# The last cross attention gets its own order of work and a ring of eight rows

## The reference, cut to what matters

```
x = x + self_attn(layernorm(x))                 # per batch item: 224 x 512
q = layernorm(x) @ Wq + bq;  k = ctx @ Wk + bk;  v = ctx @ Wv + bv      # ctx: 750 x 512
att = (q k^T / sqrt(32)) * mask - 1e10 * (1 - mask)                     # 16 heads, 224 x 750
x = x + (softmax(att) @ v) @ Wo + bo
x = x + experts(layernorm(x))      # all 8 items together, gathers rows of the expert table
```

## Time and profile before

| | |
|---|---|
| median of 3 runs | 2667.64 us (2662.12 to 3053.95) |
| the profiled execution | 2672.23 us, its span 2670.4 us |
| mean granted TensorE clock | 0.963 of full speed |
| busy share of the span | TensorE 88%, VectorE 70%, ScalarE 44%, GpSimd 42% |
| last cross attention, first scores to last quad copied | 1297.8 to 1394.2 us, 96.4 us |
| in it, granted clock | 0.77 |

### The profile page before, as it was taken

One profiled execution on the slowest core, in us unless ns is written; L12 is line 12 of the kernel. 1 busy time (PEld: TensorE's weight loads), 2 busy tenths in 40 slices (PEclk: granted clock), 3 DMA queues, 4 the chain that ended last, 5 costly groups with the idle time before them and its releaser, 6 DMA issues. The chain is left out here.

```text
span 2670.4 us, 37760 instructions
## 1 busy us (share of the span) xinstructions
PE 2355.7 (88%) x12440; PEld 1263.5 (47%) x12440; DVE 1870.6 (70%) x5466; ACT 1185.9 (44%) x3230; POOL 1122.6 (42%) x1084
## 2 busy tenths in 40 slices
PE   7899999999999999999777799898989898897777
PEld 3455564555655556555554344444444344443322
DVE  3477676776768667677554896878878787878555
ACT  1447365573745737466351343343334333433322
POOL 2121111211112111121001676777777777777775
PEclk9899999999999999999878899999999999999999
DMA  5000101001010010100202998999999999999998
GB/s 179 8 24 8 37 2 30 16 8 38 1 45 1 8 38 1 45 1 22 93 1 85 372 391 335 399 401 418 395 416 397 410 409 399 400 395 395 407 416 355
DMA packets 161362, 520.73 MB, mean 195 GB/s; under 512 B 17168, under 2 KB 27408, under 8 KB 161168
## 3 DMA queue, kind: packets, MB, share of 16 engines
q0 software_dynamic: 129024, 469.82, 44.3%
q1 hardware_dynamic: 30560, 46.98, 5.3%
q10 hardware_dynamic: 1584, 1.52, 0.2%
HBM read 507.71 MB, written 10.55 MB: 194 GB/s over the span
## 5 line engine op out<-in xcount | busy, mean ns | idle before, releaser
L1593 POOL DMA_INDIRECT e_rows<-in_experts,e_idx x896 | 888.2, 991 | 340.9 <-issue 287.7
L1650 PE MATMUL e_ps_out<-e_rows,e_diag 128*128 128x512 f32 x1792 | 843.5, 617 | 145.3 <-ACT e_diag L1917 145.1
L1811 DVE CUSTOM_DVE_ANT_0 e_rows<-e_rows,xn_all 128x512 f32<-128x512 f32 x896 | 567.8, 689 | 232.0 <-DMA e_rows<-in_experts,e_idx 231.8
L1650 PEld LDWEIGHTS e_ps_out<-e_rows,e_diag 128*128 128x128 f32 x1792 | 343.8, 197 | 594.3 <-issue 428.5
L1917 ACT ACTIVATE e_diag<-ident_f,e_weight 128x128 f32<-128x128 f32 x896 | 286.2, 390 | 313.1 <-DVE e_weight L1822 297.6
L984 DVE SCALAR_TENSOR_TENSOR ring<-ps_s,mask 112x750 f32<-112x750 f32 x256 | 232.8, 936 | 152.7 <-PE ps_s L557 115.2
L1170 ACT ACTIVATE ring<-ring,neg_max 112x750 f32<-112x750 f32 x256 | 233.4, 914 | 165.3 <-DVE neg_max L994 165.3
L568 PE MATMUL ps_t<-ident,ring 112*125 112x112 f32 x1536 | 233.6, 290 | 47.9 <-ACT prob_t L1188 36.5
L568 PEld LDWEIGHTS ps_t<-ident,ring 112*125 112x125 f32 x1536 | 199.7, 196 | 122.9 <-ACT ring L1170 61.7
L1912 ACT ACTIVATE e_active<-e_hidden 128x4 f32<-128x4 f32 x224 | 45.9, 205 | 456.4 <-DVE e_hidden L1811 456.2
L1188 ACT COPY prob_t<-ps_t 125x336 f32<-125x336 f32 x512 | 200.1, 440 | 95.6 <-PE ps_t L568 95.4
(11 more groups left out here) (186 smaller groups left out, 2850.4 us busy)
## 6 DMA issues: line engine op xcount, KB each, us to landing
e_rows<-in_experts,e_idx POOLq DMA_INDIRECT x896, 6.2
xn_t<-in_ctx_t SPq DMA_DIRECT2D x8, 1500.0 KB, 6.5
w_in<-in_ffn_wq SPq DMA_DIRECT2D x16, 256.0 KB, 6.2
acc<-in_x SPq DMA_DIRECT2D x8, 448.0 KB, 5.0
x_dram<-x SPq DMA_DIRECT2D x8, 448.0 KB, 3.1
acc<-x_dram SPq DMA_DIRECT2D x7, 512.0 KB, 6.1
out<-acc SPq DMA_DIRECT2D x14, 256.0 KB, 5.9
x2n_dram<-ring SPq DMA_DIRECT2D x7, 448.0 KB, 3.3
```

The source lines that it names most:

```text
L1593: pool.indirect_dma_start(rows[:, v % RING, k, :], None, table[:, :], bass.IndirectOffsetOnAxis(ap=idx[:, e:e + 1], axis=0))\
L1650: mm = nc.tensor.matmul(ps_out[t % 2][:], diag[:, HU * (v % ND) + k, :], rows[:, v % RING, k, D:], start=(s == 0 and k == 0), stop=(s == S ...
L1811: last = nc.vector.tensor_tensor_reduce(down, down, xn_all[:, t, :], 1.0, 0.0, ALU.mult, ALU.add, hidden[:, b, k:k + 1])
```

## The change

Three things change, all in the last batch item.

- `cross(b, following)` on TensorE, VectorE and ScalarE now serves only the first seven items. The last has a function of its own, `last_cross`, on each of the three engines. TensorE issues a quad's first scores as the quad's first work, takes the last row of the quad before out of turn, and puts `cross_weigh` behind it. VectorE takes rows and masks in pairs. ScalarE alternates exponentials and copies. Of the 12 tiles turned ahead, VectorE copies six and ScalarE six.
- The last cross attention uses eight rows: six of `ring` and two in the memory of `w_v`, which the last `values_group` has read by then (`spare`, `cross_rows`, `ring_rows`). `spread_out` and `cross_bank` give the tail other banks, so that `cross_out` of tile 1 does not wait for tile 0's `residual_2`, and `spread_sums` goes ahead of the last `cross_weigh`.
- `with_bias` of the last item waits until both tiles of the turned rows are in `act_t`.

```
-NRING, NSELF = 6, 12
+NRING, NLAST, NSELF = 6, 8, 12
...
+        spare = w_v[:].rearrange("p c n -> p (c n)")[0:TT, 0:(NLAST - NRING) * SC].rearrange("p (i n) -> p i n", n=SC)
...
-            return ((bank[2], bank[3]), ps_t)[k][t]
+            return ((bank[2], bank[3]) if k == 0 or b == last else ps_t)[t]
...
+        def ring_rows(b):
+            return NLAST if b == last else NRING
+        def cross_bank(b, t):
+            return bank[0] if b == last and t == 1 else ps_y
+        def cross_rows(b, u, n):
+            i = u % ring_rows(b)
+            return ring[:, i:i + n, :] if i < NRING else spare[:, i - NRING:i - NRING + n, :]
...  TensorE
+            def last_cross():
+                for ready in q2_ready:
+                    pe.wait_ge(ready.sem, ready.at(last, KC // 2))
+                for q in range(NQ + 1):
+                    u = 4 * q - 4
+                    if q < NQ:
+                        cross_scores(last, q, 0)
+                    if q >= 2:
+                        cross_turn(last, u - 1)
+                    if 2 <= q < NQ:
+                        turn_ahead(2 * (q - 2))
+                    if q >= 1:
+                        cross_turn(last, u)
+                    if q >= 2:
+                        cross_weigh(last, q - 2)
+                    if q < NQ:
+                        cross_scores(last, q, 1)
+                    if 2 <= q < NQ:
+                        turn_ahead(2 * (q - 2) + 1)
+                    if q >= 1:
+                        cross_turn(last, u + 1)
+                        cross_turn(last, u + 2)
+                cross_turn(last, NU - 1)
+                spread_sums(last, 1)
+                cross_weigh(last, NQ - 1)
...  VectorE
+                for q in range(NQ + 1):
+                    u = 4 * q - 4
+                    if q >= 1:
+                        shifted(last, u)
+                        shifted(last, u + 1)
+                    if q < NQ:
+                        masked(last, q, 0, 0)
+                        masked(last, q, 0, 1)
+                    if q >= 1:
+                        shifted(last, u + 2)
+                        shifted(last, u + 3)
+                    if q < NQ:
+                        masked(last, q, 1, 0)
+                        if q >= 2:
+                            turned_ahead(2 * (q - 2) + 1)
+                        masked(last, q, 1, 1)
...  ScalarE
+                for q in range(1, NQ + 1):
+                    u = 4 * q - 4
+                    cross_exp(last, u)
+                    if q >= 2:
+                        cross_turned(last, u - 1)
+                    cross_exp(last, u + 1)
+                    if 2 <= q < NQ:
+                        turned_ahead(2 * (q - 2))
+                    cross_turned(last, u)
+                    cross_exp(last, u + 2)
+                    if q >= 2:
+                        cross_quad_out(last, q - 2)
+                    cross_turned(last, u + 1)
+                    cross_exp(last, u + 3)
+                    cross_turned(last, u + 2)
+                cross_turned(last, NU - 1)
+                cross_quad_out(last, NQ - 1)
...  GpSimd, with_bias
+                else:
+                    pool.wait_ge(act_ready.sem, act_ready.at(b, 2 * NT))
```

More of the change, by code:

```diff
@@ L305, in batch_of @@
             return view[bass.ds(b, 1)].rearrange("o p t d -> (o p) t d")
-        last = B - 1
         block = ctx.enter_context(nc.Block())
@@ L664, in cross @@
             def cross(b, following):
-                if following is not None:
-                    for t in range(NT):
-                        turn_in(following, t)
+                for t in range(NT):
+                    turn_in(following, t)
                 for ready in q2_ready:
@@ L702, in _ @@
                 middle(b + 1, b)
[L703 to L708, removed]
+            last_cross()
             pe.wait_ge(xt_ready, AHEAD_TILES)
@@ L992, in shifted @@
                 dve.sem_inc(passed_dve, 1)
-                row = ring[:, u % NRING, :]
+                row = cross_rows(b, u, 1)[:, 0, :]
                 nc.vector.tensor_tensor_reduce(row, row, mask_bias[:, t, :], -1.0, 3.4e38,
@@ L1053, in _ @@
             tail(last)
-            cross(last, None)
-            for u in range(NU - 4, NU):
-                shifted(last, u)
+            last_cross()
             inverses(last, 1)
@@ L1203, in cross @@
                             cross_turned(b, 4 * q - 4 + place)
-                        if q >= 2 and place in (0, 2) and following is None:
-                            turned_ahead(2 * (q - 2) + place // 2)
                         if (q, place) not in FRONT_FIRST:
@@ L1214, in cross @@
                         cross_quad_out(b, NQ - 2)
-                    elif following is not None:
+                    else:
                         arg_plus_one(following)
                     cross_turned(b, u)
-                    if u == NU - 2 and following is not None:
+                    if u == NU - 2:
                         keys_out(following, 6)
@@ L1231, in _ @@
                 middle(b + 1)
-            cross(B - 1, None)
+            last_cross()
         @block.gpsimd
```

50 lines of the change are left out of this document (28 added, 22 removed).

## The result

The changed kernel takes 2642.7 us (median of 5), the kernel before 2663.62 us (median of 5). The ratio is 0.9916, with a 95% interval of 0.9901 to 0.9931: 22 us less, with an interval of 18 to 26. By the bound of 2% it counts as the same. One run of each kernel (3925.47 and 3053.95 us) was disturbed and stays out of the ratio.

A forecast was written before the change was run, and what follows sets the result against it. No engine is full: the chain from engine to engine, and the half clock its gaps cost, bound the loop. Loop 22.4, tail -0.85 and GpSimd 2.8 give 24.4 us: 2667.64 - 24.4 = 2643 us, range 2635 to 2657.

The forecast's parts named there:

- The loop at full clock: Last cross attention's loop: a quad takes 8.05 us against 10.01, the first period 6.8; gain 24 us at full clock throughout.
- The clock in the steady quads: Loop's steady quads: TensorE busy 7.4 of 8.05 us, or 92%, so they run at full clock.
- Rival 1: Loop: the clock still falls as often as before, 10.2 us a quad, gain of 10 there; 2656 us, chance 0.17.
- The head: Loop's first two periods: 7 us at half clock make them 7.8 and 8.7 us, together costing 1.6 us.
- The tail: Last quad's first exponential to first output projection: 14.1 us with half clock against 12.3, a loss of 1.8 us.
- the projections: Tail: tile 1's output projection, in another bank, no longer waits for residual_2; 0.95 us gained.
- GpSimd's sum: Last item, ahead of the cross attention: moving the sum off VectorE's second normalization gives back 2.8 us.
- The ring: Score rows of the last cross attention: the extra rows cost nothing by themselves, and masks never wait for them.
- Rival 2: Full clock everywhere, head and tail too, as remaining gaps are too short to cost it; gain 28, 2640 us, chance 0.22.
- Rivals 3 and 4: Loop: 3, TensorE stuck at half clock, 2675 us, chance 0.04; 4, ScalarE and VectorE hold each other up, 2653, 0.12.

The follow-up runs named there:

- pool_only: Kernel before with one edit: GpSimd's sum for the last item waits for the turned rows; ratio 0.9976 to the kernel before.
- filled_both: Changed kernel plus idle TensorE transposes into unused bank ps_y at the loop's head and tail; ratio 0.9901 to the kernel before.
- less_work: Changed kernel with idle transposes at the head only and one of four transposes per tile ahead; periods 7.82 us, total time not comparable.
- old_filled_head: Kernel before plus 12 and 24 idle TensorE transposes behind its first and second scores; ratio 0.9989 to the kernel before.
- no_pool_wait: Changed kernel without the new wait on GpSimd's sum; ratio 0.9934 to the kernel before.
- ring8_only: Kernel before with eight score rows in the last cross attention, old order and banks; ratio 0.9999 to the kernel before.
- after_again: The changed kernel unaltered, run again beside its variants; ratio 0.9921 to the kernel before.

## Why the prediction was right, point by point

I forecast 2643 us and a gain of 24.4; the median is 2642.7, and the gain from residual sum to store 24.4 in the trace. The median of before had meanwhile moved from 2667.64 to 2663.62, so by medians it is 20.9 us, by the ratio 22 (18 to 26). The agreement to 0.3 us is partly luck, and so is the trace's: its 24.4 holds the 79.14 us of one trace of the old loop, which took 74.9 to 79.1 in the five traces of the old order with ScalarE's queue unchanged. The terms are a better test. The forecast took a change of 2% (53 us) to be about the least that a measurement of this kernel can tell; the interval here is 8 us wide.

The loop's 22.2 us have two sources. By an estimate from the traces, seven old quads at 10.0 us are 70 us, so 9.1 of the old loop's 79.14 are the clock's; the new loop takes 53.7 with the head filled and 56.9 without, so 3.2 are. The order itself gives some 16 us, and 6 come from losing the clock less. The second part is the uncertain one: no trace shows the old loop at full clock throughout, and in pool_only the old loop lost only 4.9 us.

- **The loop at full clock**: I gave 8.05 us a quad, it is 7.82. Shown by the window rows and, for what stands in the loop, by two edits: moving the weighing (8.24) and putting VectorE's copy on ScalarE (8.25). The weighing's start-to-start time is 1.28 us, where I took its busy time of 1.36, and the wait of the second turn was shorter: it starts 1.49 us after the first, not 1.6. The first period at full clock, 6.8 by my sum, is 6.83 in filled_both.
- **The clock in the steady quads**: 1.00, as taken from the earlier trace rows. Rival 1 fell, and less_work kept its clock with less work still. Rival 1's support was a misreading: the window with 0.97 begins at 1315.83, and the half clock of the head lasts until 1316.4; from there on it is 1.00. That the old order's slow quads are the clock's is argued from its two kinds of period, which go with the clock column; an edit that adds idle work alone shows it for the head only, in the new order (filled_both) and in part in the old (old_filled_head: 10.95 us in place of 11.60 at 0.76 in place of 0.50).
- **The head**: 1.6 us for the clock, measured 3.2 (filled_both). Here the first period was right (7.8 and 7.76), the second mis-sized: 8.7 against 10.06, because I took 7 us at half clock where 12.1 of the 13.65 us fell into the loop. This error and that of the steady quads cancelled, which is luck: 7.8 + 8.7 + 5 x 8.05 = 56.8 us forecast, 56.90 measured.
- **The tail**: 14.1 us forecast, 14.24 measured; half clock taken, and filled_both shows that it cost 1.9 of them. In another trace the same tail took 1.5 us more (less_work), so the agreement to 0.1 is partly luck too. For the projections I gave 0.95, it was 4.61 - 3.50 = 1.1.
- **GpSimd's sum**: 2.8 us forecast, 2.81 measured in this place, 3.1 by taking it away (no_pool_wait). In the new place (1278.90 to 1281.24) no work of VectorE lies beside it, and it costs nothing, as forecast.
- **The ring** "costs nothing" and, alone, brings nothing (ring8_only).
- **Rival 2**, full clock everywhere, did not happen by itself: the gaps at head and tail cost the clock, and the clock 5.1 us (filled_both). TensorE's gaps at the head are 1.9 us each (1288.15 to 1290.05, 1290.95 to 1292.86, by start and length of its scores), and the clock fell at 1292.1, inside the second. The Trainium skill (TensorE: Matmul & The Clock Gate, HAM oscillation) lets the clock fall in long waits between bursts of matmuls, and taken for long waits alone it makes these gaps harmless. The trace agrees on the direction, as with the two gaps filled the clock held, and differs on the length: gaps of 1.9 us were enough. One such gap need not be enough, as the projection of less_work shows.
- **Rivals 3 and 4** found nothing: TensorE left half clock within the second period, and VectorE, the fullest engine, waits 0.31 us a quad.

What the timing could not show: what the single parts are worth, down to 3 or 4 us. All variants of the changed kernel lie between 0.9901 and 0.9934. Their order rests on the traces, one each (two of the changed kernel).

## What to carry to other kernels

When no engine is full but the clock column is below 1.00, the gaps can be paid twice, once as waiting and once as half-speed matmuls behind them; shortening the chain can then return more than its waits (here about 16 us of order and 6 of clock). Follow one period of a hand-written order as a loop through all queues, with start-to-start times, and change the queues together: here ScalarE's new order alone made the kernel slower, and the ring alone did nothing. The last item of a pipelined loop, where the filler is missing, deserves an order of its own.

## What the hardware showed that I had not expected

- The old order's quads mostly come in steps, 10.0 us or 11.0 to 12.3, and their pattern differs between nearly equal kernels (loops of 74.9, 75.5, 78.7, 79.1 and 79.1 us), while the new order's five full-clock periods agree to 0.02 us. A loop that loses its clock in some quads and keeps it in others is itself a source of spread.
- The tail does the same in the new order: with the same code it took 13.44 us in three traces and 14.99 in less_work, as the clock was half for 6.8 us or 13.7.
- Work that nobody needs made the kernel's stretch 5.1 us shorter, by holding the clock.
- The same kernel takes 2664 us on one chip and 2842 on two others. The attention stage takes as long: the store of the seventh item comes at 1240.84 us in pool_only, on the first chip, and at 1238.01 in after_again, on another. The expert layer differs. The same 700 us of it in these two traces:

```profile
1800.00:2500.00 700.00, 613.76 (x1566) 279.11 (x1565) 549.80 (x2015) 254.16 (x741) 529.21 (x543) 0.98 1.02 403
```

```profile
1800.00:2500.00 700.00, 573.16 (x1407) 264.29 (x1405) 479.94 (x1760) 222.85 (x642) 468.52 (x469) 0.91 0.93 349
```

DMA moved 403 GB/s and 349 GB/s, and each engine got through fewer instructions in the second. The traces on the third chip have 346 to 350. Why is not known from these runs.
